# Down projection as seven block products with sums of blocks, in place of eight: a Strassen-Winograd scheme in an f32-by-f16-halves kernel

## The reference

```python
h = _layernorm(x, axis=-1) * (1 + cb) + sb
gate = einsum('bsh,oh->bso', h, lut[gate_idx])      # 1376 outputs
up   = einsum('bsh,oh->bso', h, lut[up_idx])
hid  = silu(gate) * up
x    = x + gb * einsum('bsh,oh->bso', hid, lut[down_idx])   # back to 512
```

## Time and profile before

| what | before |
|---|---|
| median of 3 runs | 1165.8 us (1163.17 to 1166.24) |
| span of the profiled execution | 1162.8 us |
| PE busy | 1127.7 us, 97% of the span |
| DVE busy | 705.3 us, 61% |
| ACT busy | 435.6 us, 37% |
| POOL busy | 358.1 us, 31% |
| first down matmul, end of the span | 929.94 us, 1162.8 us |

### The profile page before, as it was taken

The page is one execution under the profiler, slowest core; times in us unless marked ns, Lnnn a source line. Parts: engine busy times, 40 slices in busy tenths (PEclk is TensorE's granted clock), DMA queues, the critical chain, the costliest instruction groups (busy, mean ns, idle before and its releaser), DMA issues.

```text
span 1162.8 us, 16680 instructions
## 1 busy us (share of the span) xinstructions
PE 1127.7 (97%) x6692; PEld 531.1 (46%) x6718; DVE 705.3 (61%) x1035; ACT 435.6 (37%) x729; POOL 358.1 (31%) x331
## 2 busy tenths in 40 slices
PE   4899999999999999999999999999999999999998
PEld 2344444454444444445444444444454444444443
DVE  4788988776779677996768979677432211111111
ACT  4668788776645251424323324233142200000000
POOL 1000100002126283547525637356332211111111
PEclk9999999999999999999999999999999999999999
DMA  7940233113204541312213213031121325445441
GB/s 268 322 135 1 87 109 110 38 37 109 74 1 143 182 145 74 109 73 78 82 35 118 72 72 118 35 118 43 64 92 48 147 104 179 172 173 176 177 154 59
DMA packets 52236, 125.93 MB, mean 108 GB/s; under 512 B 5216, under 2 KB 15456, under 8 KB 47040
## 3 DMA queue, kind: packets, MB, share of 16 engines
q1 hardware_dynamic: 52160, 124.87, 30.9%
HBM read 77.15 MB, written 47.71 MB: 107 GB/s over the span
## 4 chain that ended last, share of the span: by engine, by line
PE 83%; DVE 7%; issue 4%; ACT 3%; POOL 1%; DMA 1%; SPq 0%; POOLq 0%; DVEq 0%; ACTq 0%
PE bank L1232 26%; PE bank L1234 25%; PE bank L1233 25%; PE bank L1240 2%; DVE look_buf L995 2%; PE bank L1384 1%; DVE w_ffn L995 1%; DMA w_ffn<-in_wmod 1%; PE bank L1302 1%; PE bank L1366 1%; PE bank L1345 1%; DVE h L901 1%; ACT h L617 1%; ACT shared L649 1%; DVE shared L1014 0%
## 5 line engine op out<-in xcount | busy, mean ns | idle before, releaser
L1232 PE MATMUL bank<-h,w_ffn 128*128 128x512 f16 (+1 forms) x528 | 200.6, 380 | 0.2 <-POOL h L553 0.2
L1233 PE MATMUL bank<-h,w_ffn 128*128 128x512 f16 (+1 forms) x528 | 200.3, 379 | 0.0
L1234 PE MATMUL bank<-h,w_ffn 128*128 128x512 f16 (+1 forms) x528 | 200.3, 379 | 0.0
L573 POOL TENSOR_TENSOR shared<-hid_f,shared 128x512 f16<-128x512 f32 (+1 forms) x88 | 114.1, 1296 | 273.5 <-ACT shared L780 273.4
L780 ACT ACTIVATE shared<-hid_f 128x512 f16<-128x512 f32 (+1 forms) x88 | 55.4, 630 | 259.7 <-DVE hid_f L1157 251.8
L1164 DVE SCALAR_TENSOR_TENSOR shared<-bank,sc,gb_row 128x512 f32<-128x512 f32 x32 | 24.0, 751 | 205.1 <-PE bank L1234 205.1
L1157 DVE SCALAR_TENSOR_TENSOR hid_f<-bank,sc,shared 128x512 f32<-128x512 f32 (+1 forms) x88 | 65.8, 747 | 121.5 <-issue 82.4
L1232 PE MATMUL bank<-w_ffn 128*128 128x512 f16 x320 | 121.5, 380 | 0.0
L1234 PE MATMUL bank<-w_ffn 128*128 128x512 f16 x320 | 121.3, 379 | 0.0
L1233 PE MATMUL bank<-w_ffn 128*128 128x512 f16 x320 | 121.3, 379 | 0.0
L1232 PE MATMUL bank<-arena,h 128*128 128x512 f16 x256 | 98.3, 384 | 5.6 <-issue 2.5
(11 more groups left out here) (225 smaller groups left out, 1922.8 us busy)
## 6 DMA issues: line engine op xcount, KB each, us to landing
hid_dram<-shared SPq DMA_DIRECT2D x80, 256.0 KB, 2.0
w_ffn<-hid_dram SPq DMA_DIRECT2D x8, 2560.0 KB, 9.5
xg<-in_x SPq DMA_DIRECT2D x16, 1024.0 KB, 7.2
qp_dram<-qp SPq DMA_DIRECT2D x8, 1024.0 KB, 4.9
x_dram<-xg SPq DMA_DIRECT2D x8, 1024.0 KB, 4.0
xg<-x_dram SPq DMA_DIRECT2D x8, 1024.0 KB, 4.8
out<-xg SPq DMA_DIRECT2D x7, 1024.0 KB, 11.4
qp<-qp_dram SPq DMA_DIRECT2D x6, 1024.0 KB, 5.2
```

Source lines behind the costliest of these rows:

```text
L573: pool.tensor_tensor(hid[0:m, e % HIDS, 1], hid_f[0:m, e % 2], hid[0:m, e % HIDS, 0], ALU.subtract).then_inc(hid_done, 1)
L1232: pe.matmul(dst, a_hi, b_hi, start=first, stop=False)
L1233: pe.matmul(dst, a_hi, b_lo, start=False, stop=False)
L1234: last = pe.matmul(dst, a_lo, b_hi, start=False, stop=end)
```

## The change

A unit is now 256 rows (16 units, `DOWN_UNITS`). Its left operand is cut into four blocks, A11 and A12 (first 128 rows; inner chunks 0 to 4 and 5 to 9), A21 and A22 (last 128 rows). The weights are cut likewise into inner halves and into left and right 256 columns. Four blocks of output come from seven products (`PRODUCTS`) of blocks or sums of blocks: S1 to S4 on the left, T1 to T4 on the right. Chunk 10 (96 wide) is added in the ordinary way (`rest`). A matmul now has 256 columns; a unit has 7 x 5 x 3 + 12 = 117 of them, where two tiles had 66 of 512.

- Gated values go to DRAM in f32: DVE multiplies straight into the stored buffer and waits there for that buffer's earlier store (`hid_out`). `hid_hi` and `hid_lo` are gone.
- In the last stage `b`, DVE makes T1 to T4 (`right_sums`, `right_lows`), ACT their high halves (`t_hi`), and POOL copies the unchanged weight blocks (`right_planes`). `unpack` is gone.
- For each unit, one unit ahead of PE: DVE makes S1 to S4 (`left_sums`) and the low halves of the unchanged blocks (`raw_lo`, `last_lo`), ACT the eight high halves (`left_hi`, `last_hi`), POOL the four low halves of the sums (`sum_lo`).
- Outputs share partial sums. ACT copies a partial sum out of PSUM after the products 0, 1 and 2 (`hold`), DVE one after product 4 (`left_u3`), and the rows are put together by `out_row`, scaled by `out_scale`, and added to the residual by POOL (`add_rows`).
- Scale factors of the table are powers of two smaller, so that sums fit.

In the diff (indentation cut by eight) the old bodies, and the helpers `b_plane`, `last_hi`, `last_lo` and `right_lows` (copies or subtractions, one a line) are left out, and so are the declarations.

```diff
--- before.py
+++ after.py
...
+UNIT = 2 * P
+DOWN_UNITS = BATCHES * SEQ // UNIT
...
+PRODUCTS = ((S_A11, S_B11), (S_S1, S_T1), (S_S2, S_T2), (S_A12, S_B21), (S_S3, S_T3), (S_S4, S_B22), (S_A22, S_T4))
...
+    def hid_load(u):
+        g, i, cols = u // 2, u % 2, slice(u % 2 * UNIT, u % 2 * UNIT + UNIT)
+        if i == 0:
...
+        if u >= 2:
+            sp.wait_ge(raw_low, 4 * (u - 1))
+            sp.wait_ge(left_summed, 4 * (u - 1))
+        sp.dma_start(hid_raw[i][:, 0:FC - 1], hid_dram[g][:, 0:FC - 1, cols]).then_inc(hid_in[i], 16)
+        sp.dma_start(hid_raw[i][0:TAIL, FC - 1], hid_dram[g][0:TAIL, FC - 1, cols]).then_inc(hid_in[i], 16)
...
-                sp.wait_ge(up_done, SLOT[(GROUPS - 1, 5)] + 1)
+                sp.wait_ge(tf_done, 4 * HALF_K)
+                sp.wait_ge(b_planes, 3 * HALF_K + 1)
                 hid_load(0)
-            sp.wait_ge(hid_done, e + 1)
-            sp.dma_start(hid_dram[g][0:m, j], hid[0:m, e % HIDS].rearrange("p h n -> p (h n)")).then_inc(hid_out[e % HIDS], 16)
...
+    def right_planes(jj):
+        if jj == 0:
+            wait_apart(pool, look, len(UNITS) * STEPS)
+            wait_apart(pool, up_done, SLOT[(GROUPS - 1, 0)] + 1)
+            b_plane(wt_last[0:TAIL], FC - 1, TAIL, slice(0, HID))
+        b_plane(wt[S_B11][:, jj], jj, P, slice(0, HALF_N))
+        b_plane(wt[S_B21][:, jj], jj + HALF_K, P, slice(0, HALF_N))
+        b_plane(wt[S_B22][:, jj], jj + HALF_K, P, slice(HALF_N, HID))
+    def sum_lo(u, i):
+        pool.wait_ge(left_high, 8 * u + LEFT_PARTS.index(S_S1 + i) + 1)
+        block = left[u % 2][S_S1 + i]
+        pool.tensor_tensor(block[:, 1], left_sum[i], block[:, 0], ALU.subtract).then_inc(sum_low, 1)
+    def add_rows(u, i):
+        g, t = u // 2, 2 * (u % 2) + i
+        if t == 0:
+            pool.wait_ge(x1_in[g % 2], 16 * (g // 2 + 1))
+        pool.wait_ge(y_scaled, 2 * u + i + 1)
+        pool.tensor_tensor(xg[:, g % 2, t], xg[:, g % 2, t], y_t[:, i], ALU.add).then_inc(y_done, 1)
...
+    for jj in range(HALF_K):
+        right_planes(jj)
+    for i in range(4):
+        sum_lo(0, i)
+    for u in range(DOWN_UNITS):
+        if u:
+            add_rows(u - 1, 1)
+        if u + 1 < DOWN_UNITS:
+            for i in range(4):
+                sum_lo(u + 1, i)
+        add_rows(u, 0)
+    add_rows(DOWN_UNITS - 1, 1)
...
+    def t_hi(jj):
+        if jj == 0:
+            act.wait_ge(up_done, SLOT[(GROUPS - 1, 0)] + 1)
+        for at, i in enumerate((0, 2, 1, 3)):
+            act.wait_ge(tf_done, 4 * jj + at + 1)
+            act.activation(wt[S_T1 + i][:, jj, 0], t_full[:, i], ACT.Copy).then_inc(t_high, 1)
+    def left_hi(u, which):
+        i, pos = u % 2, LEFT_PARTS.index(which)
+        if u >= 2:
+            act.wait_ge(prod_ready, 7 * (u - 2) + pos + 1)
+        elif u == 1 and pos == 0:
+            act.wait_ge(up_done, SLOT[(GROUPS - 1, 4)] + 1)
+        if which >= S_S1:
+            act.wait_ge(left_summed, 4 * u + (0, 2, 1, 3)[which - S_S1] + 1)
+            src = left_sum[which - S_S1]
+        else:
+            if pos == 0:
+                act.wait_ge(hid_in[i], 32 * (u // 2 + 1))
...
+        act.activation(left[i][which][:, 0], src, ACT.Copy).then_inc(left_high, 1)
...
+    def hold(u, k):
+        i = u % 2
+        act.wait_ge(prod_ready, 7 * u + k + 1)
+        if u >= 2:
+            act.wait_ge(row_out_done, 2 * (u - 2) + 1 if k != 1 else 2 * (u - 2) + 2)
+        src = bank[(1, 7)[i]][:, HALF_N:HID] if k == 1 else bank[(0, 6)[i]][:, 0:HALF_N]
+        dst = held_p5[:, i] if k == 1 else held_row[:, i, k // 2 * HALF_N:(k // 2 + 1) * HALF_N]
+        act.activation(dst, src, ACT.Copy, scale=c1(C_INV_D)).then_inc(row_held, 1)
...
+    stage_b(GROUPS - 1, {jj + 1: [lambda jj=jj: t_hi(jj)] for jj in range(HALF_K)})
+    for which in LEFT_PARTS:
+        left_hi(0, which)
+    last_hi(0)
+    for u in range(DOWN_UNITS):
+        more = u + 1 < DOWN_UNITS
+        if more:
+            left_hi(u + 1, S_A11)
+        hold(u, 0)
+        if more:
+            left_hi(u + 1, S_S1)
+        hold(u, 1)
+        if more:
+            left_hi(u + 1, S_S2)
+            left_hi(u + 1, S_A12)
+        hold(u, 2)
+        if more:
+            for which in (S_S3, S_S4, S_A22):
+                left_hi(u + 1, which)
+            last_hi(u + 1)
...
-        if e >= 2:
-            dve.wait_ge(hid_done, e - 1)
-        dve.scalar_tensor_tensor(hid_f[0:m, i], bank[3 + 2 * i][0:m], c1(C_HID)[0:m], silu_g[0:m, i],
+        if e >= HIDS:
+            dve.wait_ge(hid_out[e % HIDS], 16 * (e // HIDS))
+        dve.scalar_tensor_tensor(hid[0:m, e % HIDS], bank[3 + 2 * i][0:m], c1(C_HID)[0:m], silu_g[0:m, i],
                                  ALU.mult, ALU.mult).then_inc(hid_f_done, 1)
+    def right_sums(jj):
+        if jj:
+            dve.wait_ge(tf_done, 4 * jj)
+            dve.wait_ge(t_low, jj)
+        for i in range(2):
+            words = down_w[:, jj + i * HALF_K]
+            dve.tensor_tensor(w_full[:, i], words[:, :, 0], words[:, :, 1], ALU.add).then_inc(wf_done, 1)
+        w1, w2 = w_full[:, 0], w_full[:, 1]
+        left_n, right_n = slice(0, HALF_N), slice(HALF_N, HID)
+        dve.wait_ge(wf_done, 2 * jj + 2)
+        dve.tensor_tensor(t_full[:, 0], w1[:, right_n], w1[:, left_n], ALU.subtract).then_inc(tf_done, 1)
+        dve.tensor_tensor(t_full[:, 2], w2[:, right_n], w1[:, right_n], ALU.subtract).then_inc(tf_done, 1)
+        dve.wait_ge(tf_done, 4 * jj + 1)
+        dve.tensor_tensor(t_full[:, 1], w2[:, right_n], t_full[:, 0], ALU.subtract).then_inc(tf_done, 1)
+        dve.wait_ge(tf_done, 4 * jj + 3)
+        dve.tensor_tensor(t_full[:, 3], w2[:, left_n], t_full[:, 1], ALU.subtract).then_inc(tf_done, 1)
...
+    def left_sums(u):
+        r = hid_raw[u % 2]
+        k1, k2 = slice(0, HALF_K), slice(HALF_K, 2 * HALF_K)
+        a11, a12, a21, a22 = r[:, k1, 0:P], r[:, k2, 0:P], r[:, k1, P:UNIT], r[:, k2, P:UNIT]
+        dve.wait_ge(hid_in[u % 2], 32 * (u // 2 + 1))
+        if u:
+            dve.wait_ge(sum_low, 4 * u)
+        dve.tensor_tensor(left_sum[0], a21, a22, ALU.add).then_inc(left_summed, 1)
+        dve.tensor_tensor(left_sum[2], a11, a21, ALU.subtract).then_inc(left_summed, 1)
+        dve.wait_ge(left_summed, 4 * u + 1)
+        dve.tensor_tensor(left_sum[1], left_sum[0], a11, ALU.subtract).then_inc(left_summed, 1)
+        dve.wait_ge(left_summed, 4 * u + 3)
+        dve.tensor_tensor(left_sum[3], a12, left_sum[1], ALU.subtract).then_inc(left_summed, 1)
+    def raw_lo(u, which):
+        i = u % 2
+        dve.wait_ge(left_high, 8 * u + LEFT_PARTS.index(which) + 1)
+        k = slice(0, HALF_K) if which == S_A11 else slice(HALF_K, 2 * HALF_K)
+        src = hid_raw[i][:, k, P:UNIT] if which == S_A22 else hid_raw[i][:, k, 0:P]
+        dve.tensor_tensor(left[i][which][:, 1], src, left[i][which][:, 0], ALU.subtract).then_inc(raw_low, 1)
...
+    def left_u3(u):
+        i = u % 2
+        dve.wait_ge(prod_ready, 7 * u + 5)
+        dve.wait_ge(row_held, 3 * u + 2)
+        dve.scalar_tensor_tensor(held_u3[:, i, HALF_N:HID], bank[(0, 6)[i]][:, 0:HALF_N], c1(C_INV_D), held_p5[:, i],
+                                 ALU.mult, ALU.add).then_inc(u3_held, 1)
+    def out_row(u, k):
+        i = u % 2
+        dve.wait_ge(prod_ready, 7 * u + 6 + k)
+        dve.wait_ge(row_held, 3 * u + 3)
+        if u:
+            dve.wait_ge(y_done, 2 * (u - 1) + k + 5)
+        if k:
+            dve.wait_ge(u3_held, u + 2)
+        src = bank[(0, 6)[i] if k else (1, 7)[i]]
+        dve.scalar_tensor_tensor(y_t[:, k], src[:], c1(C_INV_D), held_u3[:, i] if k else held_row[:, i],
+                                 ALU.mult, ALU.add).then_inc(row_out_done, 1)
+    def out_scale(u, k):
+        dve.wait_ge(row_out_done, 2 * u + k + 1)
+        dve.tensor_tensor(y_t[:, k], y_t[:, k], gb_row[:, u // (DOWN_UNITS // BATCHES)], ALU.mult).then_inc(y_scaled, 1)
...
+    def right_step(i):
+        if 2 <= i <= HALF_K + 1:
+            right_lows(i - 2)
+        if 1 <= i <= HALF_K:
+            right_sums(i - 1)
+        if i == HALF_K + 2:
+            dve.memset(held_u3[:, :, 0:HALF_N], 0.0).then_inc(u3_held, 1)
+    def left_part(u, half):
+        if half == 0:
+            left_sums(u)
+            raw_lo(u, S_A11)
+            raw_lo(u, S_A12)
+        else:
+            raw_lo(u, S_A22)
+            last_lo(u)
...
-                {j: [lambda j=j: unpack(j)] for j in range(FC)} if s == GROUPS - 1 else {})
-    for g in range(GROUPS):
-        for t in range(TILES):
-            y_tile(g, t)
+                {i: [lambda i=i: right_step(i)] for i in range(FC)} if s == GROUPS - 1 else {})
+    left_part(0, 0)
+    left_part(0, 1)
+    for u in range(DOWN_UNITS):
+        if u:
+            out_row(u - 1, 1)
+            out_scale(u - 1, 1)
+        if u + 1 < DOWN_UNITS:
+            left_part(u + 1, 0)
+        left_u3(u)
+        if u + 1 < DOWN_UNITS:
+            left_part(u + 1, 1)
+        out_row(u, 0)
+        out_scale(u, 0)
```

(63 more changed lines are left out.)

131 lines of the change are left out of this document (58 added, 73 removed).

## The result

The changed kernel takes 1179.7 us (median of 4 runs, 1179.08 to 1183.79) against 1164.5 (1163.15 to 1166.24): the ratio is 1.0136, 95% interval 1.0115 to 1.0158: 1.4% slower. The profiled execution spans 1178.5 us, 15.7 more than before.

A forecast was written before the change was run, and what follows sets the result against it. PE's matmuls were taken to bound the kernel before, DVE and POOL sharing a port after. Start 5.7, down products 8.0, last stage 3.8, tail 0.8: +18.3 on 1162.8, span 1181.1, plus 3.0: 1184 us, range 1158 to 1206.

The forecast's parts named there:

- PE's part: Down products: 117 matmuls of 0.109 us, 12.75 us a unit, 204.0 for 16, 24.1 us less than 228.1.
- T = 14.8 by turns at the read port: Each down unit takes 14.8 us because DVE's and POOL's SBUF operations exclude each other; T 14.0 to 15.8, chance 0.60.
- The first rival: Down products: DVE and POOL overlap after all, PE is the bound, time 1148 us; chance 0.15.
- T = 14.0 of the second: Rival for the down units: DVE and POOL only half exclusive, no last-stage stall, 1169 us; chance 0.12.
- The loop through PE: Down units: ACT's hold after product 2 waits behind S2 and A12, then products 4 to 6 follow: 14.6 us.
- The start: Before the first down matmul: S1 to S4 and A11's low half must come first, gap 7.4 for 1.76, +5.7 us.
- Unit 0: First down unit: its hold 1 and 2 stand behind S1 and S2 of unit 1, so it takes 16.1 us.
- The clock: Rival: PE's clock falls in each down unit after idling, T about 16.3, time 1205 us; chance 0.08.
- The last stage b: Last stage b: DVE's right sums plus turns with POOL's sixteen copies delay PE by 3.8 us, between 0 and 8.
- Edits at no cost: Removing `hid_hi` and `hid_lo` wins nothing; DVE's store wait and SP's loads are hidden.
- The tail: After the last down product: `out_scale` between `out_row` and POOL's addition adds 0.8 us.

The follow-up runs named there:

- e5: Changed kernel with the four low halves of the sums moved from POOL to DVE and unit 0's left operands prepared beside stage b's last chunks: 1147.3 us.
- e1: Changed kernel with each POOL low half of S1 to S4 replaced by two zero fills, so POOL only writes there: 1145.5 us.
- e3: Changed kernel with the four low halves of S1 to S4 moved from POOL to DVE: 1154.4 us.
- e7: Against e3, the low halves of S3 and S4 go back to POOL; those of S1 and S2 stay on DVE: 1160.4 us.
- e2: Changed kernel with ACT making hold 2 before it rounds S2 and A12 of the next unit: 1175.3 us.
- e8: Changed kernel with the edits of e2, e3 and e4 together: 1145.0 us.
- e6: Against e5, POOL's 16 copies of the weights' halves are released about three us sooner: 1145.6 us.
- e10: Against e9, POOL gets one unused 128x512 subtraction after each gated value of the first stage b: 1144.6 us.
- e9: Against e8, POOL's copies of the weights' halves are released sooner too: 1143.2 us.
- e4: Changed kernel with unit 0's left operands prepared beside the last chunks of stage b: 1173.1 us.

## Why the prediction was right

The time was forecast at 1184 and is 1179.7. Of the 4.4 us between, 2.6 are in the span, and 1.8 come from the 3.0 us by which the median of before stood above its profiled span, which are 1.2 here. The 2.6 are small in part by luck: errors of -3.4, -1.9 and +3.0 stand against each other (below). The steps, as the prediction had them:

- **PE's part** was right in the step, 0.109 us for 256 columns. A unit without a wait takes 12.78 (e5) to 12.82 (e1) and not 12.75, so some 23 us of matmul time went, not 24.1.
- **T = 14.8 by turns at the read port**: right, 14.78 and 14.84 at the full clock. e1 takes the reads away and the unit is 12.82; e3 moves them to one engine and it is 13.42; e7 in between, 13.89. In the middle units DVE's 640-element operations take 1.39 us in the mean and POOL's 1.94, where near 1.5 to 2 and near 2 was written. The Trainium skill ("SBUF — State Buffer", section "Who interferes with whom") says that of a VectorE instruction with two SBUF inputs and a GpSimd instruction that reads SBUF, the second to issue waits until the first is through. By that rule, the traces of the down products agree, but for an edge of about 0.2 us a pair (0.81 + 1.26 against the 1.88 of L1301). The first rival (overlap) falls with these, and so does T = 14.0 of the second. The wait came before product 4 and on `hold`, as written. e2 shows that this place was not the cause: moved, the unit stays 14.8.
- **The loop through PE**, put at 14.6, was close enough to T to be mistaken for it; e2 and e8 separate them.
- **The start**, +5.7: measured +5.47. Unit 0 was put at 16.1 and took 15.43: its copies of partial sums did not hold PE, but the first 5.5 us of its matmuls ran at half speed.
- **The clock** was a rival at 0.08, and it came true in part. In the idle 7.2 us before the first down matmul the granted clock falls to 0.5, the 1.2 GHz level, and stays there from 929.15 to 939.39; later it falls four times for 3.4 us, at 1018, 1049, 1079 and 1110. Such a unit takes 15.69 in place of 14.84: of the 1.7 us lost 0.8 come out of the wait. Four times 0.87 is the 3.5 us by which units 1 to 14 (210.8 us) exceed fourteen of 14.8. The rival's own loss, 1.5 in every unit, did not occur. The down products so took 239.0, forecast 236.1.
- **The last stage b** is the step whose mechanism failed. It said that POOL's copies (0.8 each) and DVE alternate, and lateness of 10.6 makes 3.8. The trace has two gaps, 1.9 in all; the copies take 0.61, mostly run before DVE's sums begin, and hold DVE once, for the rest of the train. e6 takes away that one meeting, and the gaps go with it.
- **Edits at no cost** hid a gain. "So nothing is won" overlooked the places where POOL's queue, not PE's columns, was late: `hid_lo` stood ahead of `xn`, and POOL's `qn` took turns with a DVE that came later. The step at 413.84 shrank by 1.2 and that at 381.84 by 0.7; e10 brings back 0.7 and 0.6 of them. Some 1.4 more of the 3.4 us is a fall of the clock at 268 us that the profiled execution of before has and this one has not. The row for it was on record in the earlier trace rows, read only as evidence of the clock, not as a term of the span.
- **The tail**, +0.8: measured +0.73.

Of the error of the span (forecast +18.3, measured +15.7), -3.4 is the early stages, -1.9 the last stage, +3.0 the down products, -0.2 the start, -0.1 the tail.

## What to carry to other kernels

Before work is given to an idle GpSimd, ask what VectorE does at that moment: if both read SBUF (VectorE with two inputs), the time of the two adds up, and the work is cheaper on VectorE, whose instruction is shorter (0.81 us against 1.39 for 640 f32 elements, each unhindered). Put GpSimd's reads beside VectorE's reads of PSUM, or in one block before VectorE's reads of SBUF begin (e6). A saving of matmul time counts only as far as the engines that feed the operands fit in the shorter unit: here PE needs some 23 us less, and the down products gained 17 of them (211.0 in place of 228.05, e9) only when the unit fell from 14.8 to 13.3.

## What was not expected of the hardware

A train of sixteen GpSimd copies without a pause held a two-input VectorE instruction for 3.6 us, to the train's end, while single tensor_tensor instructions of the two engines alternate (1.88 and 1.78, 2.02 and 1.98). Why no turn fell between two copies is open. GpSimd fills, which only write, cost VectorE nothing (e1). With idle stretches of 2.0 us in each 14.8 the clock fell in four of fourteen units (changed kernel) and in three (e4); with gaps of 1.2 and 0.8 it did not fall (e2).
